# One of two transposes of inverse sums removed from TensorE, the query block's weights scaled by GpSimd instead

## The reference

```
qkv = (x @ Wqkv + bqkv)                      # x is the normalised input
...
scores = jnp.einsum('bhnqd,bhnkd->bhnqk', qb, kwin) * scale   # 16 heads of 32, blocks of 128 queries
...
mask = (jnp.abs(kpos - qpos) <= W) & (kpos >= 0) & (kpos < S)
attn = jax.nn.softmax(scores, axis=-1)       # over 3 x 128 keys
out = jnp.einsum('bhnqk,bhnkd->bhnqd', attn, vwin)
return out @ Wout + bout
```

## Time and profile before

| | |
|---|---|
| three runs | 2527.32, 2529.84, 2531.0 us; median 2529.84 |
| the profiled execution | 2528.54 us, of which the span of instructions is 2526.7 us |
| PE busy | 2464.2 us (98% of the span) |
| DVE, ACT, POOL busy | 1573.3, 1460.5, 339.0 us |
| attention, mean of a step in the steady part | 10.59 us (42.34 us for four) |

### The profile page before, as it was taken

How to read it: one execution, slowest core, us unless ns; L and a number is a source line. 1 busy time by engine, 2 the same in 40 slices (tenths; PEclk the granted TensorE clock), 3 DMA queues, 4 the chain that set the end, 5 groups by cost and what they waited for, 6 DMA issues and landing times.

```text
span 2526.7 us, 57183 instructions
## 1 busy us (share of the span) xinstructions
PE 2464.2 (98%) x20512; PEld 2026.9 (80%) x20512; DVE 1573.3 (62%) x4395; ACT 1460.5 (58%) x3748; POOL 339.0 (13%) x595
## 2 busy tenths in 40 slices
PE   6999999999999999989999999999999999999996
PEld 4788888888888888868888888888888888888885
DVE  5444444444444444436777777777777777777775
ACT  6333333333333333336777777777777777777774
POOL 1011111111111111111111111111111111111111
PEclk9999999999999999999999999999999999999998
DMA  4522222222222222114777777778777777777775
GB/s 173 167 84 84 83 74 70 80 83 75 83 83 75 83 78 80 51 45 114 200 198 201 199 201 194 202 198 204 199 202 199 197 201 201 201 201 201 201 192 147
DMA packets 587918, 366.78 MB, mean 145 GB/s; under 512 B 21760, under 2 KB 542976, under 8 KB 587184
## 3 DMA queue, kind: packets, MB, share of 16 engines
q1 hardware_dynamic: 587552, 363.68, 53.1%
q0 software_dynamic: 144, 0.17, 0.0%
HBM read 197.04 MB, written 166.72 MB: 144 GB/s over the span
## 4 chain that ended last, share of the span: by engine, by line
PE 50%; ACT 2%; issue 1%; DMA 1%; DVE 1%; SPq 0%; POOLq 0%; POOL 0%; ACTq 0%; DVEq 0%
PE job_ps L1167 14%; PE job_ps L1176 7%; PE job_ps L1185 7%; PE pT_ps L1252 7%; PE job_ps L1280 7%; PE score_ps L1238 7%; ACT wqkv_raw L970 1%; PE pT_ps L1257 1%; ACT pT L980 0%; DMA wqkv_raw<-turned_blocks 0%; DMA turned_blocks<-wqkv_raw 0%; DVE wqkv_raw L1054 0%; PE job_ps L1300 0%; PE score_ps L1290 0%; ACT q_hi L996 0%
## 5 line engine op out<-in xcount | busy, mean ns | idle before, releaser
L970 ACT ACTIVATE wqkv_raw<-wqkv_raw,neg_max 128x384 f32<-128x384 f32 (+1 forms) x1024 | 619.7, 607 | 329.1 <-DVE neg_max L1054 328.9
L494 ACT ACTIVATE relu<-up_ps,fc_scale 128x512 f32<-128x512 f32 x256 | 176.3, 689 | 656.2 <-PE up_ps L625 656.2
L568 DVE SCALAR_TENSOR_TENSOR sq<-up_ps,relu 128x512 f32<-128x512 f32 x256 | 177.1, 692 | 531.7 <-ACT relu L494 530.4
L1054 DVE CUSTOM_DVE_ANT_0 wqkv_raw<-score_ps,mask 128x384 f32<-128x384 f32 (+1 forms) x1024 | 503.2, 547 | 4.0 <-PE score_ps L1238 2.2
L635 PE MATMUL down_ps<-proj_T,sq_hi 128*128 128x512 f32 x1024 | 409.2, 400 | 0.9 <-DVE sq_lo L551 0.9
L637 PE MATMUL down_ps<-proj_T,sq_lo 128*128 128x512 f32 x1024 | 404.6, 395 | 0.0
L621 PE MATMUL up_ps<-f_xT_hi,fc_T 128*128 128x512 f32 x1024 | 399.5, 390 | 1.4 <-DVE low L539 1.4
L623 PE MATMUL up_ps<-f_xT_lo,fc_T 128*128 128x512 f32 x1024 | 399.6, 390 | 0.0
L1167 PE MATMUL job_ps<-xT_hi,wqkv_hi 128*128 128x256 f32 x1024 | 330.7, 323 | 0.1
L1071 DVE STREAM_TRANSPOSE wqkv_raw<-wqkv_raw 128x384 f32<-128x384 f32 (+1 forms) x512 | 278.2, 561 | 45.7 <-ACT wqkv_raw L970 42.1
L1167 PE MATMUL job_ps<-xT_hi,wqkv_lo 128*128 128x256 f32 x1024 | 289.9, 283 | 0.0
(11 more groups left out here) (131 smaller groups left out, 4190.8 us busy)
## 6 DMA issues: line engine op xcount, KB each, us to landing
turned_blocks<-wqkv_raw SPq DMA_DIRECT2D x124, 768.0 KB, 4.6
wqkv_raw<-turned_blocks SPq DMA_DIRECT2D x496, 192.0 KB, 3.6
xT_hi<-xT SPq DMA_DIRECT2D x65, 256.0 KB, 4.8
xT_lo<-xT SPq DMA_DIRECT2D x65, 256.0 KB, 4.8
f_x_in<-in_L_attn_x SPq DMA_DIRECT2D x64, 256.0 KB, 3.1
xT<-f_xT_hi SPq DMA_DIRECT2D x64, 256.0 KB, 2.6
xT<-f_xT_lo SPq DMA_DIRECT2D x64, 256.0 KB, 2.8
part_in<-in_L_attn_x SPq DMA_DIRECT2D x64, 256.0 KB, 3.6
```

Source lines behind the costliest of these rows:

```text
L568: nc.vector.scalar_tensor_tensor(sq[:, s % 2, :], up_ps[:, s % 2, :], 0.0, relu[:, s % 2, :], ALU.max, ALU.mult).then_inc(sq_done, 1)
L970: nc.scalar.activation(probs[:, u, cols], probs[:, u, cols], ACT.Exp, bias=neg_max[:, u:u + 1], scale=-1.0, accum_out=prob_sum[:, u:u + 1] ...
L1054: nc.vector.tensor_tensor_reduce(out=probs[:, u, cols], in0=score_ps[:, h, cols], in1=mask[:, cols], scale=-SCORE_SCALE, scalar=3e38, op0= ...
```

## The change

The inverse sums of block 1 (the block that PE turns) no longer go through PE. POOL multiplies each head's weights of block 1 by that head's inverse sum, in place, one instruction of 128x384 a head (`normalise`), and PE's transposes wait for that. DVE takes the inverse sums of block 1 in two instructions of two heads, the first ahead of `scale_oT`. `scale_oT` takes its factors from a tile of its own, `factors`, of three blocks: ones, the transposed inverse sums of block 0, ones. ACT copies the transposed sums there in an instruction of their own, ahead of the copy of head 3, and the copies of heads 2 and 3 shrink from 512 to 384 columns.

```
-                nc.scalar.copy(pT[:, h, seen.start:last, :].rearrange("p w t -> p (w t)"),
-                               pT_ps[:, h % 2, seen.start * P:last * P]).then_inc(pT_done, 1)
+                if h == HC - 1:
+                    act.wait_ge(ones_set, 1)
+                    nc.scalar.copy(factors[:, 1, :], pT_ps[:, h % 2, 3 * P:4 * P]).then_inc(factors_done, 1)
+                nc.scalar.copy(pT[:, h, seen.start:seen.stop, :].rearrange("p w t -> p (w t)"),
+                               pT_ps[:, h % 2, seen.start * P:seen.stop * P]).then_inc(pT_done, 1)
...
+            def normalise(t):
+                i, _ = where(t)
+                cols = window(i, 1)
+                for u in range(HC, 2 * HC):
+                    pool.wait_ge(rcp_done, 3 * t + 2 + (u - HC) // 2)
+                    nc.gpsimd.tensor_scalar(probs[:, u, cols], probs[:, u, cols], sum_rcp[:, u:u + 1], None, ALU.mult
+                                            ).then_inc(normalised, 1)
...
                 if t < STEPS:
-                    widen_inverse_sums(t, 0)
+                    widen_inverse_sums(t)
                 if job_a(t) is not None and where(job_a(t))[0] % 2 == 0:
                     copy_keys(job_a(t))
                 if t < STEPS:
-                    widen_inverse_sums(t, 1)
+                    normalise(t)
...
                     find_max(t, 1)
+                if t < STEPS:
+                    inverse_sums(t, HC, 2)
                 if 1 <= t <= STEPS:
                     scale_oT(t - 1)
                 if t < STEPS:
-                    inverse_sums(t, 1)
+                    inverse_sums(t, HC + 2, 2)
                 if 1 <= t <= STEPS:
                     oT_low(t - 1)
...
-                pe.wait_ge(exped, 8 * t + u + 1)
+                pe.wait_ge(normalised, HC * t + h + 1)
...
-                if h >= HC - 2:
-                    place = h - (HC - 2)
-                    pe.wait_ge(rcp_widened, 2 * t + 2)
+                if h == HC - 1:
+                    pe.wait_ge(rcp_widened, t + 1)
                     last = nc.tensor.transpose(pT_ps[:, h % 2, 3 * P:4 * P],
-                                               rcp_wide[:, at(i, place), :, :].rearrange("p h t -> p (h t)"), ident[:, :])
+                                               rcp_wide.rearrange("p h t -> p (h t)"), ident[:, :])
```

More of the change, by code:

```diff
@@ L704, in attention_stage @@
         pT_moved = wqkv_raw[:, 2, :].rearrange("p (w q h t) -> p w q h t", q=STRIPS, h=HC, t=DH)
-        pT = sb("pT", [P, HC, 4, P], F32)
-        rcp_wide = sb("rcp_wide", [P, 2, HC, DH], F32)
+        pT = sb("pT", [P, HC, 3, P], F32)
+        rcp_wide = sb("rcp_wide", [P, HC, DH], F32)
+        factors = sb("factors", [P, 3, P], F32)
         oT = sb("oT", [P, T], F32)
@@ L730, in attention_stage @@
         rcp_done = sem("rcp_done")
-        rcp_widened = sem("rcp_widened")
+        rcp_widened, normalised = sem("rcp_widened"), sem("normalised")
+        ones_set, factors_done = sem("ones_set"), sem("factors_done")
         blocks_turned, blocks_out, blocks_moved = sem("blocks_turned"), sem("blocks_out"), sem("blocks_moved")
@@ L911, in _ @@
             identity_on_pool(pool, nc, ident, zeroed, ident_done)
+            nc.gpsimd.memset(factors[:, :, :], 1.0).then_inc(ones_set, 1)
             nc.gpsimd.memset(mask[:, :], 0.0).then_inc(zeroed, 1)
@@ L922, in _, with widen_inverse_sums @@
             pool.wait_ge(bias_added, 1)
-            def widen_inverse_sums(t, b):
-                pool.wait_ge(rcp_done, 2 * t + b + 1)
+            def widen_inverse_sums(t):
+                pool.wait_ge(rcp_done, 3 * t + 1)
                 if t >= 1:
                     pool.wait_ge(turned, HC * t)
-                heads = slice(b * HC, (b + 1) * HC)
-                nc.gpsimd.tensor_copy(rcp_wide[:, b, :, :], sum_rcp[:, heads].unsqueeze(2).to_broadcast([P, HC, DH])
+                nc.gpsimd.tensor_copy(rcp_wide[:, :, :], sum_rcp[:, 0:HC].unsqueeze(2).to_broadcast([P, HC, DH])
                                       ).then_inc(rcp_widened, 1)
+            def normalise(t):
[5 more added lines that the diff above has]
+                                            ).then_inc(normalised, 1)
             def copy_keys(u):
@@ L975, in copy_pT @@
                 seen = blocks_seen(i, 1)
-                last = 4 if h >= HC - 2 else seen.stop
                 act.wait_ge(turned, 4 * t + h + 1)
@@ L1056, in find_max, with inverse_sums @@
                                                    accum_out=neg_max[:, u:u + 1]).then_inc(maxed, 1)
[L1058 to L1062, removed]
+            def inverse_sums(t, first, count):
+                heads = slice(first, first + count)
+                dve.wait_ge(exped, 8 * t + first + count)
+                if t >= 1 and first == 0:
+                    dve.wait_ge(rcp_widened, t)
+                if t >= 1 and first > 0:
+                    dve.wait_ge(normalised, HC * t)
                 nc.vector.reciprocal(sum_rcp[:, heads], prob_sum[:, heads]).then_inc(rcp_done, 1)
@@ L1075, in scale_oT @@
             def scale_oT(t):
+                i, _ = where(t)
+                place = at(i, 0)
+                dve.wait_ge(factors_done, t + 1)
                 dve.wait_ge(pv_done, t + 1)
@@ L1080, in scale_oT @@
                                         job_ps[:, pv_bank(t), 0:T].rearrange("p (b t) -> p b t", t=P),
-                                        pT[:, HC - 2:HC, 3, :], ALU.mult).then_inc(oT_scaled, 1)
+                                        factors[:, 1 - place:3 - place, :], ALU.mult).then_inc(oT_scaled, 1)
             def oT_low(t):
@@ L1134, in _ @@
                         turn_blocks(t, u)
-                    inverse_sums(t, 0)
+                    inverse_sums(t, 0, HC)
                 if job_a(t) is not None:
```

## The result

The changed kernel takes 2536.56 us (median of 6 runs, 2535.58 to 2539.52); the kernel before takes 2529.2 us (median of 6, 2527.32 to 2531.05). The ratio is 1.0031, with a 95% interval of 1.002 to 1.0042: slower by 7.4 us. The forecast was 2540.7 us, slower, with 2535 to 2552 as its own range. The time and the direction came as forecast. The reason did not, as the first look at POOL shows.

A forecast was written before the change was run, and what follows sets the result against it. PE and the DVE-ACT loop were taken as level. That loop's 42.12 us a round, -0.32 for ACT, + 4 x 0.22 for the `oT_lo` hold, gave 42.68 against 42.34: +10.9 us, 2540.7 us; range 2517 to 2570, own range 2535 to 2552.

The forecast's parts named there:

- What bounds the kernel: Whole round: PE and the loop of DVE and ACT are level within half a per cent, 42.12 against 42.34 us.
- PE, 0.10 us a step: PE's transposes: one fewer in each step saves 0.10 us a step, 0.40 a round.
- ACT, -0.08: ACT's three copies ahead of `qk_high`: 0.86 us after the change, 0.08 less a step, -0.32 us a round.
- DVE's further reciprocal, nothing: DVE ahead of `scale_oT`: one more reciprocal of 0.18 us or less, hidden by 0.81 us of idle time.
- POOL, 0.51 us a multiplication: POOL's four multiplications of 128x384: 0.51 us each, from copies and casts; upper bound 0.98 from the two-input addition.
- third rival: PE's transposes of head 2 or 3 wait for POOL, each 0.1 us costing 13 us; unlikely, within a shared 0.17.
- if `oT_lo` gets in first: Where `oT_lo` and POOL's third multiplication meet on SBUF: `oT_lo` starts first and changes by -0.09 us.
- hidden: PE's transposes of heads 2 and 3: POOL finishes before they are due, so the new wait costs nothing.
- The hold of oT_lo, +0.22: `oT_lo` on DVE: POOL's 384-column instruction, reading SBUF, delays it 0.22 us more a step, on the loop to `find_max`.
- its own rival without it: At `oT_lo`: POOL does not hold DVE longer; -0.34 us a round, -11 us, 2519; chance 0.26.

The follow-up runs named there:

- e11: The kernel before, with only `add_out` moved behind `find_max(t, 0)` on DVE: 2510.44 us, ratio 0.9925.
- e1: The changed kernel without POOL's multiplications, the weights of block 1 left undivided: 2516.84 us, ratio 0.9953 to the kernel before.
- e5: The changed kernel with each POOL multiplication written with two inputs, the second the repeated column of inverse sums: 2531.81 us, ratio 1.0013 to the kernel before.
- e7: The changed kernel with a plain 128x384 copy onto itself in place of each POOL multiplication: 2539.01 us, ratio 1.0042 to the kernel before.
- e2: The changed kernel with POOL's multiplications written to a scratch tile nobody reads, PE not waiting for them: 2519.1 us, ratio 0.9961 to the kernel before.
- e6: e4 with each POOL multiplication written with two inputs, the second the repeated column of inverse sums: 2583.22 us, ratio 1.0217 to the kernel before.
- e9: The changed kernel with a constant factor of 0.25 in place of the column of inverse sums in POOL's multiplications: 2536.84 us, a single execution.
- e4: The changed kernel with block 1's first inverse sum taken earlier, between the third and fourth `find_max`, the second's ahead of `scale_oT`: 2517.17 us, ratio 0.995.

## Why the time was right and the reason wrong

The time came right by luck: the forecast counted a hold that wasn't there and left out a wait of nearly the same size.

*What bounds the kernel* (level loops): right. e11 takes `add_out` from the loop of DVE and ACT and gives 18.9 us to a kernel whose PE is busy 98% of the span, and leaves PE's work as it is.

*PE, 0.10 us a step*: right, 0.11 and 0.12 in c0 and c1 of e1. *ACT, -0.08*: it is -0.05. *DVE's further reciprocal, nothing*: right; `scale_oT` starts 0.11 us behind it, and DVE still idles 0.67 us after it.

*POOL, 0.51 us a multiplication*: this is the step that failed. It was 1.24. The rows chosen were those of copies and casts, which do no arithmetic, and the bound from above, 0.98 from the addition of two inputs, was no bound: a multiplication by a column of factors takes 1.24 us, one with that column as a repeated second input 0.83 (e5). The prediction gave the condition of its third rival, over 1.0 us for each multiplication. Its own times put it higher: from 1839.2 to head 3 near 1844.1 there is room for four of about 1.22. At 1.24 POOL and PE are about level, and the 0.25 us that POOL loses in the collision comes on top; that the loser could be POOL was a case that the prediction had ("if `oT_lo` gets in first"), but it put no cost on POOL's side. What it called hidden was PE's wait, and that is what the time went into.

*The hold of oT_lo, +0.22*: absent in the changed kernel (0.446 us in the median, 0.07 less than before), present in e7, where POOL's instruction takes 0.51 us, at 0.20. The prediction's chain from there to the time is confirmed by e7: 42.68 us a round forecast and measured, 10.9 us over the kernel before forecast and 10.8 measured; the small errors of the hold (0.20 for 0.22) and of ACT (-0.05 for -0.08) nearly cancel. So the forecast is right for a kernel with the price that it assumed. For this kernel two errors met. The hold was worth some 22 us in the forecast, 2540.7 against 2519 in its own rival without it, and it wasn't there; a wait of 17.5 us was, and had not been counted. They left 4 us between them. That the time was in the range is not evidence for the reason given, and the trace and e2 show another.

## What to carry to other kernels

Where one engine is busy nearly all the time, look for the loop through the others before counting what it is spared; here a move of one 0.6 us instruction on DVE was worth 19 us, and the removed transpose with the shorter copies 12. For work given to an idle engine, work out when it starts and when each piece is due, with the price of just that kind of instruction. If no row has that price, a row of another kind is no upper bound for it, and the case in which the piece comes late needs a cost and a chance of its own. Where two engines may collide, ask what it costs either of them. When a start is what matters, release the first piece alone: the same POOL work, begun half a microsecond earlier and so out of the collision, turned a loss of 7 us into a gain of 12.

## What the runs showed of the hardware

On POOL, float32, 384 columns in SBUF: a copy 0.51 us, a multiplication with a repeated second input 0.83, a multiplication by a constant 1.17, by a column of factors 1.24 (0.93 for 256 columns).

The next table shows how POOL's instruction and `oT_lo`, a DVE instruction with two SBUF inputs, meet. Starts and ends are those of POOL's instruction, measured from the start of `oT_lo`, which takes 0.425 us when alone:

| kernel | POOL instruction | starts | ends | oT_lo longer by |
|---|---|---|---|---|
| before | copy, 128 columns | -0.05 | 0.24 | 0.09 |
| e5 | two inputs, 384 | -0.46 | 0.36 | 0.22 |
| e7 | copy, 384 | -0.07 | 0.44 | 0.29 |
| e6 | two inputs, 384 | -0.05 | 0.78 | 0.63 |
| e9 | by a constant, 384 | -0.10 | 1.07 | 0.25 |
| e4 | by a column, 384 | -0.52 | 0.72 | 0.00 |
| changed kernel | by a column, 384 | -0.01 | 1.48 | 0.02 |

In the first four rows, copies and instructions of two inputs, POOL is ahead and `oT_lo` is held until 0.14 to 0.15 us before POOL's instruction ends, so for nearly all of it. The Trainium skill (SBUF — State Buffer, section Who interferes with whom) says that the loser waits for the whole instruction; the prediction read one row, 0.09 us, as speaking against that, and with three more the rule fits these rows, less a constant 0.15. For the multiplications by a factor it doesn't hold: `oT_lo` is free where one has run for 0.52 us (e4), and is held by 0.25 us where one has run for 0.10 and has 1.07 left (e9); and in the changed kernel, with a lead of 0.01 us, POOL is the one that is held, by 0.25 us (1.49 against 1.24). The rows of e4 and e9 would fit an instruction that holds `oT_lo` during its first half microsecond alone: by the reckoning of the first four rows e9's hold ends 0.10 + 0.25 + 0.15 = 0.50 us after POOL's start, an estimate, and e4's `oT_lo` comes at 0.52. No run puts the meeting elsewhere, so this is not shown.
